# Layer 0's attention: the biased score tiles in pairs of heads, with bias tiles of 64 rows

## The reference

```python
q, k, v = (split_heads(x @ W + b) for W, b in ((Wq, bq), (Wk, bk), (Wv, bv)))
energy = jnp.einsum('bhqd,bhkd->bhqk', q, k)
rel = pos[:, None] - pos[None, :] + (N - 1)          # N = 1024
rel = jnp.clip(rel, 0, bias_table.shape[0] - 1)      # the table has 249 rows
energy = energy + bias_table[rel].transpose(2, 0, 1)[None]
att = jax.nn.softmax(energy / (scaling * temp), axis=-1)
out = jnp.einsum('bhqk,bhkd->bhqd', att, v)
return out.transpose(0, 2, 1, 3).reshape(B, N, C) @ Wp + bp
```

## Time and profile before

| | us |
|---|---|
| median of 3 runs | 1306.81 |
| the 3 runs | 1306.81, 1296.58, 1309.57 |
| the profiled execution | 1299.84 |
| its span, first to last instruction | 1297.9 |

### The profile page before, as it was taken

One profiled execution on the slowest core, in us unless ns is written; L12 is line 12 of the kernel. 1 busy time (PEld: TensorE's weight loads), 2 busy tenths in 40 slices (PEclk: granted clock), 3 DMA queues, 4 the chain that ended last, 5 costly groups with the idle time before them and its releaser, 6 DMA issues.

```text
span 1297.9 us, 18539 instructions
## 1 busy us (share of the span) xinstructions
PE 1126.3 (87%) x6826; PEld 526.3 (41%) x6826; DVE 808.7 (62%) x1582; ACT 649.2 (50%) x1246; POOL 193.0 (15%) x309
## 2 busy tenths in 40 slices
PE   5599999799899999999875792899999799897777
PEld 3366666222222322322123341434443367643344
DVE  6633333789598899887038581878785235465554
ACT  4332322157587777778524251656777522334344
POOL 2145653000010010010100000102231000001000
PEclk9699999679799999999677575979999899999888
DMA  4521224132101101100004432111023310000331
GB/s 140 180 84 50 89 89 88 49 76 70 45 23 35 35 19 35 43 11 18 10 10 127 146 65 68 44 35 36 29 89 107 105 56 1 1 1 1 131 131 33
DMA packets 62165, 77.93 MB, mean 60 GB/s; under 512 B 15760, under 2 KB 39936, under 8 KB 60032
## 3 DMA queue, kind: packets, MB, share of 16 engines
q1 hardware_dynamic: 62080, 76.81, 19.5%
HBM read 61.58 MB, written 14.56 MB: 59 GB/s over the span
## 4 chain that ended last, share of the span: by engine, by line
PE 68%; DVE 13%; SPq 6%; DMA 5%; ACT 5%; issue 2%; POOL 0%; DVEq 0%; ACTq 0%
PE PS L1496 66%; DVE mx L1289 5%; ACT arena L883 4%; SPq L532 3%; DMA sums<-arena 2%; DMA arena<-k_dram 1%; SPq L539 1%; SPq L550 1%; DVE arena L1470 1%; PE PS L1509 1%; DMA arena<-drev_dram 1%; DVE arena L1103 1%; DVE arena L1106 0%; DMA arena<-mrow 0%; DVE small L1456 0%
## 5 line engine op out<-in xcount | busy, mean ns | idle before, releaser
L1496 PE MATMUL PS<-arena 128*32 128x512 f32 (+13 forms) x3656 | 621.1, 491 | 72.6 <-DVE mx L1289 38.7
L883 ACT ACTIVATE arena<-PS 128x512 f32<-128x512 f32 (+3 forms) x896 | 438.7, 557 | 270.0 <-PE PS L1496 266.1
L1289 DVE TENSOR_REDUCE mx<-PS 128x1 f32<-128x512 f32 (+3 forms) x896 | 506.8, 625 | 103.0 <-PE PS L1496 99.1
L1496 PEld LDWEIGHTS PS<-arena 128*32 128x32 f32 (+3 forms) x3656 | 159.3, 105 | 444.5 <-DVE mx L1289 178.7
L1496 PE MATMUL PS<-x_hi,w_hi_lo 128*128 128x512 f32 x320 | 144.9, 495 | 1.2 <-DVE fw L1390 0.8
L1390 DVE TENSOR_TENSOR fw<-PS,fw 128x512 f32<-128x512 f32 x80 | 55.3, 692 | 119.7 <-ACT fw L930 117.9
L930 ACT ACTIVATE fw<-PS 128x512 f32<-128x512 f32 x80 | 47.8, 597 | 123.5 <-PE PS L1496 123.5
L821 POOL TENSOR_TENSOR fw<-fw,arena 128x512 f32<-128x512 f32 x64 | 84.9, 1327 | 88.9 <-DVE fw L1390 88.9
L1496 PE MATMUL PS<-fw 128*128 128x512 f32 (+3 forms) x184 | 90.3, 578 | 0.0
L774 POOL TENSOR_TENSOR arena<-arena,fw 128x512 f32<-128x512 f32 x32 | 41.0, 1281 | 265.5 <-DMA fw<-sum_dram 265.5
L1496 PEld LDWEIGHTS PS<-x_hi,w_hi_lo 128*128 128x128 f32 x320 | 61.0, 191 | 31.2 <-issue 19.5
(11 more groups left out here) (281 smaller groups left out, 1030.2 us busy)
## 6 DMA issues: line engine op xcount, KB each, us to landing
arena<-comb_dram SPq DMA_DIRECT2D x16, 1024.0 KB, 5.2
fw<-sum_dram SPq DMA_DIRECT2D x32, 256.0 KB
arena<-comb_dram SPq DMA_DIRECT2D x16, 512.0 KB, 7.3
arena<-k_dram SPq DMA_DIRECT2D x16, 408.0 KB
q_dram<-arena SPq DMA_DIRECT2D x24, 256.0 KB, 3.7
k_dram<-arena SPq DMA_DIRECT2D x24, 256.0 KB, 3.8
arena<-q_dram SPq DMA_DIRECT2D x16, 384.0 KB
arena<-drev_dram SPq DMA_DIRECT2D x32, 192.0 KB, 3.6
```

The source lines that it names most:

```text
L883: s.activation(Pr[:, m % 8, 0:w], bank(4 + m % 3, 0, w), ACT.Exp).then_inc(A["e_done"], 1)
L1289: v.reduce_max(mx[:, H % 2, kh, n:n + 1], bank(U % RING, 0, w), axis=AX.X, negate=True).then_inc(A["ring_free"], 1)
L1496: return nc.tensor.matmul(out_, lhsT, rhs, start=start, stop=stop)
```

## The change

In layer 0 the biased tiles of two heads (j = 0 and 1, or 2 and 3) are now made together. `flip` and `Hst` are cut to 64 contraction rows, so that the bias of head j lies in the same half of the partitions as its Q and K. A 128-row product becomes two of 64 rows (`half` 0 and 1), each of which gives one half of the anti-diagonal's side: 64 output rows in S, 64 output columns in T. So every bias matmul becomes two, and those of the two heads alternate.

```diff
@@ s_plan
+    if layer == 0:
+        marks = [n + first_of_pair(stream[n - 1]) for n in marks]
...
-            while i < len(steps) - 1 and done * t_total >= total * t_done:
+            while i < len(steps) - 1 and done * t_total >= total * t_done and not (layer == 0 and second_of_pair(what)):
@@ sync
             def load_bias(G):
                 parity = G % 2
                 for j in range(HG):
-                    src = bass.AP(tensor=drev_dram.tensor, offset=G * (HG * PARTS * DREV) + j * PARTS * DREV,
-                                  ap=[[1, P], [DREV, PARTS], [1, 256]])
-                    sp.dma_start(Hst[:, parity, j, :, :], src).then_inc(h_ld[parity], 16)
+                    row = 64 * (j % 2)
+                    src = bass.AP(tensor=drev_dram.tensor, offset=(G * HG + j) * 2 * PARTS * DREV,
+                                  ap=[[1, 64], [DREV, 2 * PARTS], [1, 256]])
+                    sp.dma_start(Hst[row:row + 64, parity, j // 2, :, :], src).then_inc(h_ld[parity], 16)
...
-                    dst = drev_dram[b * NG:(b + 1) * NG, :, part, :].rearrange("g j n -> (g j) n")
-                    sp.dma_start(dst, dpart[:, part, :]).then_inc(drev_stored, 16)
+                    for half in range(2):
+                        dst = drev_dram[b * NG:(b + 1) * NG, :, half, part, 0:DREV - 64 * half].rearrange("g j n -> (g j) n")
+                        sp.dma_start(dst, dpart[:, part, 64 * half:DREV]).then_inc(drev_stored, 16)
@@ gpsimd
+                    (flip_sw, [[1, P]], -(P // 2 - 1), 1, ALU.not_equal, 1.0),
...
+                    (flip_sw[:, :], [[1, P]], -(P + P // 2 - 1), 1, ALU.not_equal, 1.0),
@@ tensor, attention
+                def flip_of(row, half):
+
+                    return (flip, flip_sw)[(half + row // 64) % 2][row:row + 64, :]
...
-                        for part in range(PARTS):
-                            ins = mm(bank(U % RING, h0, 512), flip[:, :], Hst[:, G % 2, j, part, 0:512 - h0], start=False, stop=part == PARTS - 1)
+                        for part in range(PARTS):
+                            for half in range(2):
+                                rows = slice(64 - 64 * half, P - 64 * half) if (part, half) != (PARTS - 1, 1) else slice(0, P)
+                                pieces.append((dst[rows, h0:512], flip_of(row, half)[:, rows], Hst[row:row + 64, G % 2, pr, PARTS * half + part, 0:512 - h0]))
...
+                def add_in_turn(adds, done):
+
+                    for n in range(len(adds[0])):
+                        for dst, weights, moving in (adds[0][n], adds[1][n]):
+                            ins = mm(dst, weights, moving, start=False, stop=n == len(adds[0]) - 1)
+                            if n == len(adds[0]) - 1:
+                                ins.then_inc(done, 1)
...
+                        elif first_of_pair(what):
+                            other = what[:2] + (what[2] + 1,) + what[3:]
+                            assert place[l][other] == U + 1
+                            dst2 = bank((U + 1) % RING, 0, what[5])
+                            if U >= RING:
+                                pe.wait_ge(A["ring_free"], U - RING + 1)
+                            s_main(what, dst, False)
+                            if U + 1 >= RING:
+                                pe.wait_ge(A["ring_free"], U - RING + 2)
+                            s_main(other, dst2, False)
+                            add_in_turn((adds, s_adds(other, dst2)), A["ring_full"])
...
+                                for half in range(2):
+                                    cols = slice(64 - 64 * half, P - 64 * half)
+                                    pieces.append((dst[:, q * P + cols.start:q * P + cols.stop],
+                                                   Hst[row:row + 64, G % 2, pr, PARTS * half + part, x0:x0 + P], flip_of(row, half)[:, cols]))
...
+                    elif j % 2 == 0:
+                        st_main(H, i, j, False)
+                        st_main(H, i, j + 1, False)
+                        add_in_turn((adds, st_adds(H, i, j + 1, bank(4 + (m + 1) % 3))), A["st_ps"])
```

More of the change, by code:

```diff
@@ L128, in s_stream, with first_of_pair, second_of_pair @@
     return stream + [(name, K) for name, K, k in late], ends
+def first_of_pair(what):
+    return what[0] == "S" and what[2] % 2 == 0
+def second_of_pair(what):
+    return what[0] == "S" and what[2] % 2 == 1
 def two_halves(layer, H):
@@ L1553, in attention, with s_adds @@
                 A = att[l]
-                def mask(out_, row, weights, moving):
-                    for n, (w_, m_) in enumerate(zip(weights, moving)):
-                        ins = mm(out_, w_[row:row + 64, :], m_[row:row + 64, :], start=False, stop=n == 1)
-                    return ins
-                def s_unit(U, what):
+                def flip_of(row, half):
+                    return (flip, flip_sw)[(half + row // 64) % 2][row:row + 64, :]
+                def s_adds(what, dst):
@@ L1563, in s_unit @@
                     _, H, j, q, kh, w = what
                     G, pr, row = H // 2, j // 2, 64 * (j % 2)
-                    dst = bank(U % RING, 0, w)
-                    biased = l == 0 and q < 2 and kh == 1
-                    masked = l == 1 and q // 4 == kh
-                    ins = mm(dst, Qs[G][row:row + ROWS, pr, q * P:(q + 1) * P], Ks[G][row:row + ROWS, pr, 512 * kh:512 * kh + w],
-                             stop=not (biased or masked))
-                    if biased:
+                    if l == 0 and q < 2 and kh == 1:
@@ L1571, in s_unit @@
                         h0 = 256 if q == 0 else 384
+                        pieces = []
                         for part in range(PARTS):
-                            ins = mm(bank(U % RING, h0, 512), flip[:, :], Hst[:, G % 2, j, part, 0:512 - h0], start=False, stop=part == PARTS - 1)
-                    if masked:
-                        order = (identb, identb_sw) if row == 0 else (identb_sw, identb)
-                        masks = (mask_kq, mask_kq_sw) if row == 0 else (mask_kq_sw, mask_kq)
-                        ins = mask(bank(U % RING, w - P, w), row, masks, order)
@@ new lines, in s_adds, with s_main @@
+                    return []
+                def s_main(what, dst, alone):
+                    _, H, j, q, kh, w = what
+                    G, pr, row = H // 2, j // 2, 64 * (j % 2)
+                    return mm(dst, Qs[G][row:row + ROWS, pr, q * P:(q + 1) * P], Ks[G][row:row + ROWS, pr, 512 * kh:512 * kh + w], stop=alone)
+                def add_in_turn(adds, done):
[4 more added lines that the diff above has]
+                                ins.then_inc(done, 1)
@@ L1604, in ring_unit, with st_adds, st_main @@
                                             ident[:, :]).then_inc(A["ring_full"], 1)
-                def st_step(H, i, j):
+                def st_adds(H, i, j, dst):
                     kt, off = t_steps(l, H)[i]
                     G, h, pr, row = H // 2, H % 2, j // 2, 64 * (j % 2)
+                    wide = range(1 if kt == KT - 2 else 2) if l == 0 and h == 0 and kt >= KT - 2 else ()
+                    if wide:
+                        pieces = []
+                        for q in wide:
+                            x0 = P * (len(wide) - 1 - q)
+                            for part in range(PARTS):
[3 more added lines that the diff above has]
+                                                   Hst[row:row + 64, G % 2, pr, PARTS * half + part, x0:x0 + P], flip_of(row, half)[:, cols]))
+                        return pieces
+                    if l == 1 and kt * P == 512 * h + off:
+                        return [(dst[:, 0:P], o_[row:row + 64, :], m_[row:row + 64, :])
+                                for o_, m_ in zip(*((identb, identb_sw), (mask_kq, mask_kq_sw)) if row == 0 else
+                                                  ((identb_sw, identb), (mask_kq_sw, mask_kq)))]
+                    return []
+                def st_main(H, i, j, alone):
+                    kt, off = t_steps(l, H)[i]
+                    G, pr, row = H // 2, j // 2, 64 * (j % 2)
                     m = HG * (steps_before(l, H) + i) + j
```

61 lines of the change are left out of this document (34 added, 27 removed).

## The result

| | before | after |
|---|---|---|
| median of 22 runs each, us | 1307.40 (1296.58 to 1318.73) | 1299.58 (1289.00 to 1305.86) |
| profiled execution, us | 1299.84, span 1297.9 | 1297.81, span 1295.6 |

The ratio is 0.9946, 95% interval 0.9923 to 0.9969: 7.8 us faster by the medians, between 4 and 10 by the interval. The forecast was 1288 us and 15 us of gain; the time lies in the stated range (1274 to 1302), but only half of the gain came.

What follows compares the result with a forecast made beforehand. TensorE was taken to set the pace where the bias is, VectorE elsewhere. Savings of 12.3 us (seven periods), 1.5 and 1.2 (the ends) made 15.0, from 1299.84 to 1284.8; 3 added gave 1288 us, range 1274 to 1302.

Runs made afterwards that it cites:

- e10_best: e6_s_pairs_fill2 with the last 14 S tiles and last maxima of layer 0 moved earlier: 1276.39 us, ratio 0.9767 to the kernel before.
- e6_s_pairs_fill2: Kernel after with T tiles one at a time, S tiles in pairs, and two added matmuls a step in the T-only stretches: 1277.26 us, ratio 0.9771.
- e1_s_pairs: Kernel after with each biased T tile made alone, S tiles still in pairs: 1292.45 us, ratio 0.9896 to the kernel before.
- e5_fill4: Kernel after with four added matmuls a step, into a bank nobody reads, in the T-only stretches: 1307.99 us, ratio 0.9989 to the kernel before.

## What to carry to other kernels

Compare a rearrangement with the plainest form of the same idea, not only with the old code: here half the rows without pairs gave 1.0 of 1.1 us a group, pairing one kind of tile gave another 1.1 and pairing the other kind took 1.0 away. When a producer finishes two things at once, ask whether its consumer now starts late and the next buffer becomes a wait, as both kinds of pairs did here; walk that wait through every step, also behind the one that is rearranged. And where TensorE has only light work at the half clock, compare the stretch with a run in which it has more to do. Compare whole times at a like mean clock: here that turned 7.8 us into 10.

## What the runs showed of the hardware

- Layer 0's last half, T tiles alone, stays at the clock 0.50 for 28.6 us with PE busy 26.8 of them; with two matmuls more in a step, busy throughout, the clock is back 10 us after its fall. The same kind of work at the full clock can also stay there: layer 1's last half had 1.00 in before (PE busy 22.1 of 25.9 us) and 0.53 in after. At 1.2 GHz (0.50) a step takes 3.7 us; at 2.4 GHz (1.00) it takes 2.6 in e10_best, even with two matmuls more.
- The Trainium skill (TensorE: Matmul & The Clock Gate, HAM oscillation) describes the fall of the clock in a wait for a transfer. The trace of e6_s_pairs_fill2 agrees: TensorE waits from 600.38 to 605.11 for the maxima's transfer, and the clock is 1.00 up to 604 and 0.50 from there. That light but steady work can then go on at the half clock for tens of microseconds is what these runs add.
- 64-column matmuls with a weight load each start every 29 ns in one half of the rows, and a 512-column matmul in the other half starts among them (379.04 and 379.05 in e1_s_pairs).
- From the start of an exponential of 512 columns (0.60 us) to the weight load that waited for its end it is 0.65 us in both places read: 411.95 to 412.60 before, 396.51 to 397.16 after.
- Going from 51-row to 128-row matmuls or back costs TensorE 0.10 us: in e5_fill4 such neighbours start 0.32 us apart instead of 0.22.
